# First attention of a conv-attention hybrid: every second item keeps whole fp32 probabilities, where it was every fourth

## The reference, cut to what matters

```python
# first attention, per image: xf is [64, 1024]
q, k, v = wq @ xf, wk @ xf, wv @ xf          # [32, 1024] each
att = softmax(k.T @ q, axis=2)               # 1024 x 1024
out = x + wo @ (att @ v.T).T
...
# second attention: t is [4, 1024, 64], causal, 8 heads of 64
t = t + (softmax(mask(q @ k.T / 8)) @ v) @ Wo   # q, k, v from layernorm(t)
...
# then t + sigmoid recurrence over batchnorm(layernorm(t) @ W.T)
```

## Time and profile before

| what | value |
|---|---|
| median of three runs | 568.92 us |
| lowest and highest run | 566.38 and 571.42 us |
| span of the profiled execution, first to last instruction | 567.0 us |
| the profiled execution's own time | not listed by itself; the median stands 1.92 us above the span |
| PE, ACT, DVE, POOL busy in the span | 490.0, 429.3, 398.8, 424.4 us |
| first attention's scores (L511), first and last | 22.3 and 109.4 us |
| granted TensorE clock, mean of the span | 0.974 |

### The profile page before, as it was taken

The page is one execution under the profiler, slowest core; times in us unless marked ns, Lnnn a source line. Parts: engine busy times, 40 slices in busy tenths (PEclk is TensorE's granted clock), DMA queues, the critical chain, the costliest instruction groups (busy, mean ns, idle before and its releaser), DMA issues.

```text
span 567.0 us, 16744 instructions
## 1 busy us (share of the span) xinstructions
PE 490.0 (86%) x6771; PEld 323.0 (57%) x6771; DVE 398.8 (70%) x909; ACT 429.3 (76%) x832; POOL 424.4 (75%) x463
## 2 busy tenths in 40 slices
PE   4699978988799998889999988998999999787783
PEld 1277655655565755565666756565666766564431
DVE  5878888767678786576767676766767786328757
ACT  3488867866778878587888878787888878785593
POOL 3867965857988797968788797899788799985002
PEclk9999999989999999799999999999999999998698
DMA  9100000000000000000000000000000000000001
GB/s 230 68 3 2 2 20 1 4 1 3 1 22 2 3 3 2 3 1 21 2 3 2 4 3 1 21 3 1 1 3 3 2 3 2 2 2 2 0 2 74
DMA packets 3580, 7.46 MB, mean 13 GB/s; under 512 B 1168, under 2 KB 1456, under 8 KB 3376
## 3 DMA queue, kind: packets, MB, share of 16 engines
q1 hardware_dynamic: 3056, 5.34, 3.5%
q10 hardware_dynamic: 448, 1.05, 0.6%
HBM read 4.22 MB, written 1.05 MB: 9 GB/s over the span
## 4 chain that ended last, share of the span: by engine, by line
PE 45%; DVE 22%; POOL 17%; ACT 9%; issue 6%; DMA 1%; DVEq 0%; SPq 0%; POOLq 0%; ACTq 0%
POOL probs_low L1250 10%; PE bank L537 9%; DVE attn_partial_max L903 7%; ACT probs_high L779 6%; PE bank L497 6%; PE bank L570 5%; PE bank L574 4%; DVE conv_partial_max L897 3%; PE bank L578 3%; PE bank L576 3%; PE bank L455 2%; PE bank L522 2%; PE bank L483 2%; PE bank L456 2%; POOL tokens L1260 2%
## 5 line engine op out<-in xcount | busy, mean ns | idle before, releaser
L1250 POOL TENSOR_TENSOR probs_low<-probs,probs_high 128x512 f16<-128x512 f32 x288 | 327.6, 1158 | 77.5 <-ACT probs_high L779 76.7
L775 ACT ACTIVATE probs<-bank 128x512 f32<-128x512 f32 x352 | 214.7, 611 | 84.2 <-PE bank L537 69.0
L903 DVE TENSOR_REDUCE attn_partial_max<-bank 128x1 f32<-128x512 f32 (+2 forms) x288 | 185.3, 685 | 99.5 <-PE bank L497 99.0
L779 ACT ACTIVATE probs_high<-bank 128x512 f16<-128x512 f32 x288 | 176.8, 614 | 0.0
L574 PEld LDWEIGHTS bank<-values_high,probs_high 128*128 128x128 f16 x1152 | 105.7, 98 | 74.2 <-issue 35.8
L574 PE MATMUL bank<-values_high,probs_high 128*128 128x65 f16 x1152 | 128.8, 196 | 15.5 <-POOL probs_low L1250 11.4
L576 PE MATMUL bank<-values_low,probs_high 128*128 128x64 f16 x1152 | 127.6, 194 | 0.0
L578 PE MATMUL bank<-values_high,probs_low 128*128 128x65 f16 x1152 | 127.1, 194 | 0.0
L576 PEld LDWEIGHTS bank<-values_low,probs_high 128*128 128x128 f16 x1152 | 106.9, 99 | 3.2
L578 PEld LDWEIGHTS bank<-values_high,probs_low 128*128 128x128 f16 x1152 | 107.2, 98 | 0.0
L570 PE MATMUL bank<-values,probs 128*128 128x65 f32 x512 | 71.7, 278 | 0.8 <-POOL probs_low L1250 0.8
(11 more groups left out here) (192 smaller groups left out, 708.9 us busy)
## 6 DMA issues: line engine op xcount, KB each, us to landing
x_channels<-in_x_cm SPq DMA_DIRECT2D x6, 256.0 KB, 7.6
tokens<-in_x_tm SPq DMA_DIRECT2D x1, 1024.0 KB, 10.4
out<-ln_channels SPq DMA_DIRECT2D x4, 256.0 KB, 2.0
attn_weights<-in_attn_w ACTq DMA_DIRECT2D x1, 512.0 KB, 6.2
attn_keys_split<-attn_keys_high SPq DMA_DIRECT2D x4, 128.0 KB, 2.3
attn_keys_split<-attn_keys_low SPq DMA_DIRECT2D x4, 128.0 KB, 2.4
queries_high<-minus_max_rows SPq DMA_DIRECT2D x32, 2.0 KB
x_channels<-in_x_cm ACTq DMA_DIRECT2D x2, 128.0 KB, 3.2
```

The lines of the kernel that those rows point to most:

```text
L775: ins = nc.scalar.activation(e32[:, i % E_RING, :], o[:], ACT.Exp, scale=scale)
L779: ins = nc.scalar.activation(p_hi[:, i % P_RING, :], o[:], ACT.Exp, scale=scale)
L903: nc.vector.reduce_max(dst, o[:].rearrange("p (n w) -> p n w", n=n), AX).then_inc(s_prep_used, 1)
L1250: nc.gpsimd.tensor_tensor(out=p_lo[:, i % P_RING, :], in0=e32[:, i % E_RING, :], in1=p_hi[:, i % P_RING, :], op=ALU.subtract).then_inc(s_r ...
```

## The change

One constant is changed. In the first attention the items with odd n are now whole; before, only n = 3, 7, 11 and 15 were. So n = 1, 5, 9 and 13 of each image, 16 of the 64 items, go from split to whole. The second attention and the order of the slots are as they were.

```diff
-CONV_WHOLE, ATTN_WHOLE = 4, 6
+CONV_WHOLE, ATTN_WHOLE = 2, 6
```

## The result

The changed kernel takes 572.38 us (median of ten runs, 570.67 to 576.29), the kernel before 569.38 us in ten runs (566.38 to 571.42). The ratio is 1.0064, interval 1.0038 to 1.0091: the change makes the kernel slower, by some 3.6 us (2.2 to 5.2); the medians alone differ by 3.0 us.

The account below looks back on a forecast made before the run. No engine bounds the kernel on average; stretch by stretch, TensorE sets the end where VectorE follows closely. The terms 0.69 + 0.2 + 0.69 - 0.26 + 0.69 + 0 + 0.67 = +2.7 us on 568.92 gave 571.6 us, range 567.0 to 576.4.

Parts of the forecast that it names:

- TensorE's price: First attention: a whole turn takes 0.84 us against 0.36 split, 0.48 us more per changed item, 7.68 us for all 16.
- VectorE's lag: From the end of TensorE's last maximum matmul to VectorE's reduction; 0.27 us in the first stretch, hiding that much of 0.96.
- The fourth stretch: 60 to 72 us: n = 9 of the second image skips GpSimd's subtraction wait at 63.98; -0.26 us, bounds -0.74 and +0.96.
- The relief of ScalarE and GpSimd at nothing: 7.5 us of exponentials and 18.0 us of subtractions removed, costed at nothing except where named, as neither engine mostly ends last.
- The second and the fourth term: Stretch 38 to 49, +0.2 us after ScalarE's relief, and stretch 60 to 72, -0.26 us from the vanished wait.
- A later start of the second attention moving all behind it: Behind the first attention everything shifts by the same amount, as orders and rings there are unchanged.
- the signs: Among them: wait at 63.98 gone, row-maxima waits shorter only in stretches four to six, last score 2 to 3 us later.
- not all is exposed: Answers the first rival: TensorE's extra work exposed everywhere in the first attention, up to 7.68 us, 576.6 us; chance 0.15.
- That relief wins: Fourth rival: GpSimd and ScalarE set the pace in more stretches, vanished waits outweigh extra matmuls; 567.9 us; chance 0.06.
- Durations as the price: Third rival: by mean durations a whole turn is no dearer than a split one, saving 2.9 us, 566.0 us; chance 0.01.
- the estimate of 81 ns a matmul: Skill's figure for TensorE turns: 0.97 us split against 0.65 whole, saving 5.1 us; works the third rival's way.
- The clock: Second rival: missing the clock fall at 122 to 124, some 1.7 us, gives 569.9 us; another fall 573.3; one fewer, chance 0.10.

Follow-up runs that it names:

- after_again: The changed kernel with no edit, run once more for a second profile; 571.5 us in one run.
- at_28_60: Kernel before with only items 1, 5, 17 and 21 made whole, in the first and third stretch; 569.46 us in one run.
- at_60_97: Kernel before with only items 25, 29, 41 and 45 made whole, behind the normalisation and in the sixth stretch; 568.63 us in one run.
- pe_only: Changed kernel with the 16 items in fp32 on TensorE but keeping both exponentials, the subtraction and its wait; ratio 1.008 to the kernel before.
- relief_only: Changed kernel with one exponential and no subtraction for the 16 items, but still 12 fp16 matmuls each; ratio 0.9953 to the kernel before.
- all_whole: Kernel before with all 64 items of the first attention whole, 48 more than before; 586.77 us in one run.

## Why the prediction was right, point by point

The forecast was +2.7 us; the stretches measure +3.40 and the runs some +3.6 us. Its terms, from `after_again`:

| stretch | forecast | measured |
|---|---|---|
| 28 to 38 | +0.69 | +0.83 |
| 38 to 49 | +0.2 | +0.31 |
| 49 to 60 | +0.69 | +0.90 |
| 60 to 72 | -0.26 | -0.37 |
| 72 to 84 | +0.69 | +0.87 |
| 84 to 97 | 0 | 0.00 |
| 97 to the first turn | +0.67 | +0.86 |

- TensorE's price, 0.48 us a turn, held for seven of the sixteen turns: 0.83 or 0.84 us where 0.84 was read, for a turn of 0.36. The other nine take 0.92 to 0.94 us, seven of them right behind another turn (such as that at 52.58) and two in the last stretch; they cost some 0.56 us each, all sixteen 8.4 us and not 7.68. The trace's weight loads (PEld) suggest why: the first load of the turn at 55.86 in `after_again`, behind a 512-column matmul, starts 0.21 us ahead of it (55.65) and that of the turn at 52.58 0.03 us ahead (52.55), while the loads follow each other 0.11 us apart in both; no run tests it. All four turns of the last stretch are among the nine, and it grew by 0.86 where 0.67 was forecast.
- That the place decides held best: `at_28_60` and `at_60_97` put nearly the same work on TensorE and differ by 1.6 us.
- VectorE's lag was sized too large. I let it hide 0.27 us of 0.96 in the first, third and fifth stretch. I had read it from the chain, whose piece starts at 37.12, where the instruction before it ends; the timeline has the reduction start at 37.04, so the lag was 0.19. Of that 0.04 remains in the changed kernel and can hide nothing, which leaves some 0.15; the wait at the end of the first stretch shows it, 0.63 before and 0.50 after. The first stretch then comes to 0.96 - 0.15 = 0.81 us, the third and the fifth, with one turn of 0.92 in each, to 1.04 - 0.15 = 0.89; they grew by 0.83, 0.90 and 0.87. These three terms are 0.53 of the 0.72 us by which the sum fell short.
- The fourth stretch: the size was near, the mechanism was not, so that the size came near is luck. I let n = 9 of the second image skip the wait for GpSimd. Where nothing is delayed ahead, that and n = 13 becoming whole shorten the stretch by 0.21 us (`at_60_97`, forecast 0.26). But in the changed kernel the wait was already gone, because TensorE came later to it: 0.42 us with no item changed there (`at_28_60`), and 12.07 us with the wait for the subtraction kept (`pe_only`). The two do not add.
- The relief of ScalarE and GpSimd at nothing: right inside the changed kernel (0.22 us by `pe_only`, all of it in the last stretch); by itself it is worth 1.5 us (`relief_only`). I took it as a fixed amount, and it is one that a dearer TensorE uses up.
- The second and the fourth term are off by 0.11 us each, one up and one down, and cancel in the sum; that is luck too.
- A later start of the second attention moving all behind it: the last addition of a half to the tokens comes 400.0 and 401.0 us after the first turn in the two profiles of the kernel before, 400.3 and 398.5 us in those of the changed kernel. Nothing is given back or lost there that the executions don't differ by anyway.
- Of the signs, the missing exponentials and subtractions and the vanished wait at 63.98 came. Three did not. The waits for row maxima shrank in the first and third stretch too (0.63 to 0.50) and not in the sixth (1.05 in both). The stretch from 72 to 84 grew by 0.87, close to the full 0.96 that I had called a sign of being wrong. And the last score of the first attention came 4.2 us later after the first transpose, not 2 to 3: the waits that paid for the last turns, at 110.72 and behind it, stand after that score.

The rivals: not all is exposed (3.4 of 7.7 us), though at `all_whole`'s dose it goes that way, 17 of 23. That relief wins is out: by itself it is worth less than the price. Durations as the price, 2.9 us faster, is refuted by the starts and by every stretch that grew. So is the estimate of 81 ns a matmul that I took from the Trainium skill's page TensorE: Matmul & The Clock Gate, section Back-to-back issue gap: a split turn has some 30 ns a matmul (0.36 us for twelve). The Trainium skill's figure is for 128 columns, and these matmuls have 64 or 65; but the eight fp16 matmuls of 128 columns from 113.19 to 113.64 in the kernel before start 56 ns apart, so it does not hold here for 128 either. The clock: a fall in the first stretch costs 1.5 to 1.7 us, the size that I had given the one from 122 to 124, whose own cost no run shows. Such falls stand in profiles of both kernels, and tell single executions apart, not the kernels.

## What to carry to other kernels

What a dearer instruction costs is set by its place: read, stretch by stretch between two hand-overs, which engine ends last, and how long the bottleneck then waits; four dearer turns, some 2 us, cost 1.4 us in one place and nothing in another. An overlap that was read from the profile before is not a fixed amount: a delay earlier in the same order can use up the wait on which a later term rests, so terms of one engine may not add. A lag is read from the starts of both instructions in the timeline, not from the pieces of a chain. Where runs scatter by 1% and a stretch repeats to a few hundredths of a microsecond, the stretches of two profiles tell more than their times, as long as the granted clock in them is the same.

## What the runs showed of the hardware that was not expected

The first stretch of the first attention ran at a clock of 1.00 in some executions and at 0.85 to 0.88 in others of the same program, and took 1.5 to 1.7 us longer in those: 10.08 and 11.75 us for the kernel before, 10.91 and 12.43 for the changed one. In the second profile of the kernel before, the granted clock is 0.50, the lower of the two levels, from 29.0 to 32.4 us. Before that stretch TensorE had worked with pauses, waiting 1.7 to 2.1 us for each of the first two row maxima. Profiles without a fall in the stretch have pauses as long (1.75 and 1.73 us in the first profile of the kernel before), so what decides is open. Further on in the first attention no profile has a fall.

Eight fp32 matmuls of 65 columns, a whole turn, took 0.84 us from their start to that of the next matmul, but 0.92 us right behind a split turn. The twelve fp16 ones took 0.36 us in both places.
